# First attention's output projection as three fp32r products over a split context, with the low part formed by VectorE

## What is computed

```
x   = x + tanh(g_xattn[0]) * attn(layernorm(x), ctx, ctx)
q   = Q @ Wq + bq ; k = K @ Wk + bk ; v = V @ Wv + bv      (256 -> 256, split in 16 heads of 16)
out = softmax(q k^T / 4) v                                  (per head)
attn = out @ Wo + bo                                        (256 -> 256: the output projection)
```

## Time and profile before

| what | value |
|---|---|
| median of 3 runs | 870.87 us (869.88 to 871.38) |
| the profiled execution's own time | 870.99 us |
| its span | 868.9 us |
| mean granted TensorE clock | 0.973 |
| PE busy | 800.8 us, 92% |
| DVE busy | 660.6 us, 76% |
| ACT busy | 591.8 us, 68% |
| POOL busy | 129.3 us, 15% |
| first attention | from the start to about 198.6 us |

### The profile page before, as it was taken

One profiled execution on the slowest core, in us unless ns is written; L12 is line 12 of the kernel. 1 busy time (PEld: TensorE's weight loads), 2 busy tenths in 40 slices (PEclk: granted clock), 3 DMA queues, 4 the chain that ended last, 5 costly groups with the idle time before them and its releaser, 6 DMA issues. The chain is left out here.

```text
span 868.9 us, 15644 instructions
## 1 busy us (share of the span) xinstructions
PE 800.8 (92%) x5417; PEld 646.1 (74%) x5419; DVE 660.6 (76%) x1511; ACT 591.8 (68%) x1224; POOL 129.3 (15%) x234
## 2 busy tenths in 40 slices
PE   5799999997877999999999999999999999996767
PEld 5577777665545887888888888888888888885223
DVE  5688888885884878877876876876876876765587
ACT  4377767665625777777777777777777777775663
POOL 4333333320000001000000000000000000000546
PEclk9699999999989999999999999999999999999788
DMA  4734443305005000000000000000000000000002
GB/s 130 134 119 143 139 128 108 102 14 159 1 0 167 13 1 1 13 1 1 13 2 1 13 1 1 14 1 2 14 1 1 1 1 1 1 2 0 1 1 97
DMA packets 40301, 33.49 MB, mean 39 GB/s; under 512 B 12624, under 2 KB 38800, under 8 KB 39968
## 3 DMA queue, kind: packets, MB, share of 16 engines
q1 hardware_dynamic: 37728, 31.63, 12.4%
q0 software_dynamic: 2496, 0.87, 0.7%
HBM read 17.46 MB, written 2.10 MB: 23 GB/s over the span
## 5 line engine op out<-in xcount | busy, mean ns | idle before, releaser
L1923 DVE TENSOR_REDUCE c_neg_max<-c_pS 128x1 f32<-128x512 f32 x128 | 88.3, 690 | 62.8 <-PE c_pS L2178 60.7
L1754 ACT ACTIVATE c_probs<-c_pS,c_neg_max 128x512 f32<-128x512 f32 x128 | 88.1, 688 | 58.7 <-DVE c_neg_max L1923 58.7
L566 DVE TENSOR_REDUCE a_neg_max<-a_pS 128x2 f32<-128x512 f32 x128 | 82.4, 687 | 28.4 <-PE a_pS L813 27.8
L1772 ACT ACTIVATE c_probs<-c_probs,c_r_sum 128x512 f32<-128x512 f32 x128 | 92.5, 722 | 3.9 <-DVE c_r_sum L1929 2.7
L410 ACT ACTIVATE a_probsT<-a_pT 128x512 f32<-128x512 f32 x128 | 70.3, 609 | 25.7 <-PE a_pT L826 25.3
L1907 DVE TENSOR_TENSOR c_pT_lo<-c_pT,c_pT_hi 128x512 fp32r<-128x512 f32 x128 | 87.1, 681 | 0.0
L2139 PE MATMUL c_pK<-c_kv,w_hi 128*128 128x512 f32 x256 | 80.6, 396 | 4.6 <-PEq L1591 4.0
L2195 PE MATMUL c_pO<-c_pT_hi,c_v_hi 128*128 128x256 f32 x256 | 77.7, 304 | 4.2 <-DVE c_pT_lo L1907 4.2
L2165 PE MATMUL c_pK<-w_hi,c_kv 128*128 128x512 f32 x248 | 79.3, 401 | 1.9 <-DVE c_k_lo L1891 1.9
L2185 PE MATMUL c_pT<-ident,c_probs 128*128 128x128 f32 x512 | 76.6, 272 | 0.0
L2185 PEld LDWEIGHTS c_pT<-ident,c_probs 128*128 128x128 f32 x512 | 63.4, 140 | 17.3 <-ACT c_probs L1772 0.6
(11 more groups left out here) (399 smaller groups left out, 2044.0 us busy)
## 6 DMA issues: line engine op xcount, KB each, us to landing
a_q_stack<-w_hi SPq DMA_DIRECT2D x94, 64.0 KB, 2.6
a_k_stack<-w_hi SPq DMA_DIRECT2D x48, 64.0 KB, 2.6
c_kv<-w_hi SPq DMA_DIRECT2D x42, 64.0 KB, 2.6
s_ctx<-in_ctx_dram SPq DMA_DIRECT2D x8, 256.0 KB, 3.7
x_sb<-in_x_dram SPq DMA_DIRECT2D x8, 256.0 KB, 4.2
b_raw<-in_L_xattn_Wkv_dram SPq DMA_DIRECT2D x1, 2048.0 KB, 10.8
ctx_in<-in_ctx_dram SPq DMA_DIRECT2D x8, 256.0 KB, 2.7
out_dram<-x_sb SPq DMA_DIRECT2D x8, 256.0 KB, 2.1
```

Source lines behind the costliest of these rows:

```text
L566: nc.vector.tensor_reduce(neg_max[:, r // 2 % 2, :, e, r % 2], pS[:, e, :, :], AX_X, ALU.max, negate=True).then_inc(s["max"], 1)
L1754: nc.scalar.activation(probs[:, u % 2, :], pS[:, u % 2, :], ACT.Exp, bias=neg_max[:, u % 4:u % 4 + 1], accum_out=sums[:, u % 4:u % 4 + 1]) ...
L1772: nc.scalar.mul(probs[:, u % 2, :], probs[:, u % 2, :], r_sum[:, u % 4:u % 4 + 1]).then_inc(s["probs"], 1)
L1923: nc.vector.tensor_reduce(neg_max[:, u % 4:u % 4 + 1], pS[:, u % 2, :], AX_X, ALU.max, negate=True).then_inc(s["max"], 1)
```

## The change

In batches 0 to 6 the output projection becomes three fp32r products for each contraction block, as in the other projections. `wo` is split once: ACT writes its high part (`wo_high`, at the end of r 7 of batch 0), DVE its low part (`wo_low`, in r 1 of batch 1, in the place where later batches do out_bias). For each batch ACT's copy to `oT_norm` now rounds to fp32r, and a new DVE operation, `onT_low`, subtracts it from bank pP. It stands in r 6 behind q_low in batches 1 to 6, and behind `slot_small` in batch 7. `out_project` waits for it and issues 12 matmuls in place of 4. `onT_out` also waits until the last projection has been done. The last batch's own projection stays float32 and takes its context from a piece of `v_ones` that is free by then. New tiles lie in memory that was already there.

```diff
--- before.py
+++ after.py
@@ -140,7 +140,11 @@
         oT = sb("a_oT", [P, 2, H0 // HG, T])
         r_sum = sb("a_r_sum", [P, TT, H0])
         o_norm = sb("a_o_norm", [P, TT, D])
-        oT_norm = sb("a_oT_norm", [P, DC * T])
+        oT_norm = sb("a_oT_norm", [P, DC * T], F32R)
+        oT_norm_lo = part(1, 5376, 512)
+        oT_last = flat(v_ones[:, 0, :, :, :].rearrange("p t h e -> p t (h e)"))[:, 0:DC * T]
+        wo_hi = [part(1, 4864 + D * c, D) for c in range(DC)]
+        wo_lo = [part(1, 5888, D), part(1, 4096, D)]
         out_b = sb("a_out_b", [P, TT, D])
 
         unit = out_b[0:2, 0, :]
@@ -155,7 +159,7 @@
         pK = pb("a_pK", [P, 512])
         pV = pb("a_pV", [P, 512])
 
-        names = """bvw bvo bo bias x0 x1 x2 x ident ident0 first_k first_q gate load_k load_q load_v load_b load_g load_o ctx next wk wq wv scale
+        names = """wo_hi wo_lo onT_lo bvw bvo bo bias x0 x1 x2 x ident ident0 first_k first_q gate load_k load_q load_v load_b load_g load_o ctx next wk wq wv scale
                    const ones zeros unit units stats moments var rstd xn cT cT_hi cT_lo xT xT_hi xT_lo k k_hi k_lo q q_hi
                    q_lo stack0 stack1 v vb S max parts turned shift shifted0 shifted1 ST exp PV oT oQ rsum on onT onT_sb wo ob res
                    small wT wT_act wT_dve hs tau mean c1 bias1 bvx gh_pre slot_stats slot_moments slot_var slot_rstd slot_xn
@@ -429,8 +433,15 @@
                     act.wait_ge(s["turned"], b * 4 + g + 4)
                 nc.scalar.copy(oT[:, par, g, :], pO[:, 0, :]).then_inc(s["oT"], 1)
 
+            def wo_high():
+                act.wait_ge(s["load_o"], 2 * DMA)
+                for c in range(DC):
+                    last = nc.scalar.copy(wo_hi[c], wo[:, c, :])
+                last.then_inc(s["wo_hi"], 1)
+
             def onT_out(m):
                 act.wait_ge(s["onT"], m + 1)
+                wait(act, s["wo"], m)
                 nc.scalar.copy(oT_norm[:, :], pP[:, :]).then_inc(s["onT_sb"], 1)
 
             def weight_out(i):
@@ -463,6 +474,8 @@
                         v_out(b + 1, 1 - par)
                     if r == 1 and prep:
                         ctxT_hi(b + 2, par, pV)
+                    if r == NR - 1 and b == 0:
+                        wo_high()
                     if r % 2 and not more:
                         weight_out(r - 1)
 
@@ -497,7 +510,7 @@
             weight_out(NTURN - 1)
             for t in range(TT):
                 act.wait_ge(s["onT"], B + t)
-                nc.scalar.copy(oT_norm[:, :].rearrange("p (c t) -> p c t", c=DC)[:, :, t * P:(t + 1) * P],
+                nc.scalar.copy(oT_last.rearrange("p (c t) -> p c t", c=DC)[:, :, t * P:(t + 1) * P],
                                onT_bank(t).rearrange("p (c t) -> p c t", c=DC)).then_inc(s["onT_sb"], 1)
 
         @block.vector
@@ -573,6 +586,16 @@
                 dve.wait_ge(s["rsum"], 2 * m + t + 1)
                 nc.vector.tensor_tensor(o_norm[:, t, :].rearrange("p (h d) -> p h d", d=DK), o[:, :, 0:DK],
                                         r_sum[:, t, :, None].broadcast_to([P, H0, DK]), ALU.mult).then_inc(s["on"], 1)
+
+            def wo_low():
+                dve.wait_ge(s["wo_hi"], 1)
+                for c in range(DC):
+                    last = nc.vector.tensor_tensor(wo_lo[c], wo[:, c, :], wo_hi[c].bitcast(F32), ALU.subtract)
+                last.then_inc(s["wo_lo"], 1)
+
+            def onT_low(m):
+                dve.wait_ge(s["onT_sb"], m + 1)
+                nc.vector.tensor_tensor(oT_norm_lo, pP[:, :], oT_norm[:, :].bitcast(F32), ALU.subtract).then_inc(s["onT_lo"], 1)
 
             def out_bias(m):
                 dve.wait_ge(s["wo"], m + 1)
@@ -660,6 +683,7 @@
                 weight_out(1)
                 residual(b - 2)
                 slot_small()
+                onT_low(b - 1)
                 weight_out(3)
                 slot_sums(1, 0)
                 slot_sums(1, 1)
@@ -685,6 +709,8 @@
                             norm_stats(b + 2)
                             norm_moments(b + 2)
                     if r == 1:
+                        if done and not old:
+                            wo_low()
                         if old:
                             out_bias(b - 2)
                         if prep:
@@ -704,6 +730,8 @@
                         k_low(b + 2, par)
                     if r == 6 and prep:
                         q_low(b + 2, par)
+                    if r == 6 and done:
+                        onT_low(b - 1)
                     if not prep and r in (0, 2):
                         slot_sums(0, r // 2)
                     if not prep and r == 4:
@@ -872,13 +900,16 @@
                 turn(pP, o_norm, "onT")
 
             def out_project(m):
-                pe.wait_ge(s["onT_sb"], m + 1)
-                if isinstance(m, int) and m == 0:
-                    pe.wait_ge(s["load_o"], 2 * DMA)
+                pe.wait_ge(s["onT_lo"], m + 1)
+                if m == 0:
+                    pe.wait_ge(s["wo_lo"], 1)
                 for t in range(TT):
+                    i = 0
                     for c in range(DC):
-                        last = nc.tensor.matmul(pP[:, t * D:(t + 1) * D], oT_norm[:, c * T + t * P:c * T + (t + 1) * P], wo[:, c, :],
-                                                start=(c == 0), stop=(c == DC - 1))
+                        for w, v in ((wo_hi, oT_norm[:, :]), (wo_hi, oT_norm_lo), (wo_lo, oT_norm[:, :])):
+                            last = nc.tensor.matmul(pP[:, t * D:(t + 1) * D], v[:, c * T + t * P:c * T + (t + 1) * P], w[c],
+                                                    start=(i == 0), stop=(i == 3 * DC - 1))
+                            i += 1
                 last.then_inc(s["wo"], 1)
 
             def weight_turn(i):
@@ -922,7 +953,7 @@
             def last_out_project(t):
                 pe.wait_ge(s["onT_sb"], B + t)
                 for c in range(DC):
-                    last = nc.tensor.matmul(out_bank(t)[:, 0:D], oT_norm[:, c * T + t * P:c * T + (t + 1) * P], wo[:, c, :],
+                    last = nc.tensor.matmul(out_bank(t)[:, 0:D], oT_last[:, c * T + t * P:c * T + (t + 1) * P], wo[:, c, :],
                                             start=(c == 0), stop=(c == DC - 1))
                 last.then_inc(s["wo"], 1)
```

## The result

| | before | changed |
|---|---|---|
| median, first timing (8 runs each) | 871.19 us (869.88 to 872.80) | 874.22 us (873.04 to 877.58) |
| ratio, 95% interval | | 1.0044 [1.0029, 1.0058] |
| profiled execution, its span | 870.99, 868.9 us | 873.04, 870.9 us |
| from batch 1's first shifted scores to the next stage's first transposition ("the rounds") | 145.05 us | 147.17 us |
| the span less the rounds ("the rest") | 723.85 us | 723.73 us |

A forecast was written before the change was run, and what follows sets the result against it. PE's list in written order was taken to set the first attention's pace. Stalls of 2.40 and 0.65, less 0.33, plus 0.10 gave +2.82 us on the profiled 870.99, 873.8; the median lies 0.12 lower, so 873.7 us, range 871.4 to 875.3.

The forecast's parts named there:

- The matmuls: Output projection on PE: twelve fp32r matmuls take 1.59 us in place of 1.92, saving 0.33 us each time.
- onT_low's own time: New DVE subtraction on 128x512: 0.681 us, starting behind q_low where the residual started.
- From its end to PE: From the end of onT_low to PE's first matmul of the projection: 0.14 us.
- Batch 3: Counted like batches 2, 4 and 5: PE stalls 0.93 us at the projection, net 0.60 us later.
- Batch 6: No q_low there, so onT_low is ready before PE arrives: no stall, -0.33 us.
- Batch 7: onT_low stands behind slot_small; PE saves 0.33 us, but DVE is the bound: +0.1 in place of -0.33.
- wo's split: ACT's two copies and DVE's two subtractions, once: both hidden; without cover 0.25 and 0.87 us.
- DVE has over 3 us idle in a batch. I count nothing.: DVE's added work pushes residual, pair_max and moments by about 0.60 us: no cost elsewhere counted.
- the argument that PE is as late as DVE: Next batch's first scores: PE and DVE both come about 0.60 us later, so the gap between them stays.
- no stall: Rival: onT_low done before PE reaches the projection; six savings, DVE adds 0.1: -1.9, 869.0 us. Chance 0.12.
- The knock-on: Rival: PE's first scores of the next batch wait for DVE's maxima, up to 0.3 us five times: 875.2 us. Chance 0.08.

The follow-up runs named there:

- e10: The kernel before, unchanged, traced and timed again: rounds 144.92 us, median 870.68 us.
- e11: The kernel before, unchanged, traced and timed once more: rounds 144.92 us, median 869.64 us.
- e5: Changed kernel, high part of the context taken twice, DVE's subtraction kept on other data with nobody waiting: rounds 146.55 us, 874.78 us, ratio 1.0040 to the kernel before.
- e2: Changed kernel with onT_low moved ahead of q_low in round 6: rounds 146.78 us, median 874.52 us, ratio 1.0040 to the kernel before.
- e1: The changed kernel again, no edit: rounds 147.14 us, median 873.98 us, ratio 1.0035 to the kernel before.
- e3: Changed kernel without onT_low or its wait, high part of the context taken twice, still twelve matmuls: rounds 144.01 us, 870.82 us, ratio 0.9996 to the kernel before.
- e6: Changed kernel with the residual moved from round 7 to the front of round 6: rounds 147.17 us, 875.29 us, ratio 1.0041 to the kernel before.
- e7: Changed kernel with both onT_low ahead of q_low and the residual early in round 6: rounds 144.30 us, 871.04 us, ratio 0.9999 to the kernel before.
- e12: Changed kernel without onT_low (high part taken twice), residual moved to the front of round 6: rounds 143.79 us, 872.08 us in one run, kernel before 869.71.
- e9: Changed kernel with the residual early in round 6 and q_low moved behind round 7's pair_max: rounds 152.20 us, 879.32 us, ratio 1.0091 to the kernel before.
- e4: Kernel before plus DVE's subtraction and PE's wait for it, float32 matmuls kept, wo not split: rounds 149.00 us, 877.02 us, ratio 1.0068 to the kernel before.
- e8: Kernel before with only the residual moved to the front of round 6: rounds 144.72 us, 870.64 us, ratio 1.0007 to the unedited kernel before.

## Why the prediction was right

The sign, the mechanism and the size of the time held: a wait of PE ahead of the projection, released by onT_low, in batches 1 to 5 and in no other, and the stage later by some 2 to 3 us. Step by step:

- *The matmuls*: 1.61 us measured for 1.59, so the saving was 0.31 and not 0.33. The estimate from the count of passes in the Trainium skill (FP8 and Floating Point Precision, TensorE Precision Notes), 1.44, was too low; three passes cost 0.84 of the float32 form here, by 1.61 over 1.92.
- *onT_low's own time*: 0.680 for 0.681, and DVE began it 0.07 us before q_low's record ended, so the residual's place was the right one to read. It took 0.60 us of DVE's list (92.14 to 92.74). The rule of the Trainium skill that I had weighed against the rows (VectorE: DVE Perf Modes, The DRAIN you can't avoid) did not show; the same section says that a next operation that nothing holds starts earlier, and with that the trace agrees, by these 0.07 us.
- *From its end to PE*: the term that was mis-sized. I took 0.14 from a projection whose first instruction waits; here it is 0.05. That is 0.09 in five batches, 0.45 of the 0.70 us by which the sum was too high.
- *Batch 3*: +0.37 in place of 0.60. The kernel before had lost 0.15 us there at the scores of round 1 (97.19 to 97.68 in place of 0.34), in all three of its traces, which the changed kernel has not. I had taken four batches as alike from their clocks at the projection alone.
- *Batch 6*: -0.45 for -0.33. In the first trace of the kernel before two instructions of round 2 took 0.15 us more than elsewhere (159.84 to 160.67 for two times 0.34); why is not known. e10 and e11 do not have it, with 17.84 and 17.83 for this batch, and against them the change gives -0.3, as forecast.
- *Batch 7*: +0.01 for +0.10. As forecast, nothing of PE's 0.31 us reached the end.
- *wo's split*: hidden, as forecast. ACT made the copies in 0.73 us behind batch 0's exponentials, and the next exponential began 0.67 after them with no wait of PE. In the changed kernel:

```profile
52.59 0.73 ACT L439 CAST w_lo<-a_wo 128x256 fp32r<-128x256 f32 x2
53.26 1.08 ACT L414 ACTIVATE a_probsT<-a_pT 128x512 f32<-128x512 f32 x2
...
55.65 0.75 DVE L593 TENSOR_TENSOR w_lo<-a_wo,w_lo 128x256 fp32r<-128x256 f32 x2
```

What I had wrong without its showing in the number is the sentence "DVE has over 3 us idle in a batch. I count nothing." In the changed kernel nothing came on top of the wait, but only just: PE came 0.85 - 0.31 = 0.54 us later in batch 2 and DVE's list was 0.60 longer, so the argument that PE is as late as DVE was off by 0.06, which was all the room there was. That it was enough was luck. The list was no cover: e5 shows that the operation costs 1.5 us without any wait. And the rival "no stall" was priced at -1.9 us; e2, which is that case, came out 1.7 us above the kernel before in its rounds. A rival's price has to be worked out through the next bound as well. The knock-on, to which I gave 0.08, is the mechanism that stood ready behind the forecast.

That the forecast of 873.7 meets the median of 874.22 so closely is luck in part: the sum was 0.7 too high for the rounds, and the medians are some 1 us further apart than the rounds.

## What to carry to other kernels

An idle share says little of an engine: what counts is how much room its list has between the instruction that releases it and the one that waits for its last result, and here that was 0.06 of 20 us. Where an operation is added at such a place, removing the wait on it gives little until the list behind it is shortened as well; look for both before judging either. Before moving an operation back, follow all its readers, DMA queues among them.

## What the runs showed of the hardware

The end of the DVE operation and the first matmul that waits for it are 0.05 us apart in the changed kernel, 0.06 at the scores of e2, and 0.14 in the rows of project_k. What makes the difference was not tried.

The granted clock behind the barrier differs from run to run of the same code. Busy time by stretch (the third number from the end is the granted clock), of the changed kernel and then of the kernel before:

```profile
199.00:204.00 5.00, 4.17 (x18) 3.80 (x19) 2.90 (x12) 3.14 (x6) 1.21 (x4) 0.66 0.58 198
200.00:201.00 1.00, 1.00 (x6) 1.00 (x6) 1.00 (x4) 1.00 (x1) 0.00 (x0) 0.50 0.40 37
```

```profile
199.00:204.00 5.00, 4.47 (x28) 3.23 (x27) 3.01 (x13) 3.74 (x7) 1.01 (x1) 1.00 0.82 313
```

In both PE had been idle 2.34 us at the barrier, and the clock goes down to 0.50, the 1.2 GHz level, in the one and stays at 2.4 GHz in the other. The next stage's first work then takes 205.81 - 199.83 = 5.98 us in place of 203.84 - 198.67 = 5.17, 0.81 us more. e1, the same kernel, stays at full clock there. Of fourteen traces seven show it: those of the changed kernel's first run, e2, e3, e5, e6, e7 and e12; it is not in e1 and e9, nor in the five of the kernel before and its variants (its first, e4, e8, e10 and e11). The same code at the barrier can thus go either way, and yet it fell on the changed kernel and its variants alone, on seven traces of nine; were it blind to the kernel, a split as uneven as this would come up about once in a hundred times (7 of 14, all among 9: 36 in 3432). When the barrier falls does not sort them: the next stage starts at 196.9 to 202.0 us in the seven and at 197.7 to 206.8 in the others. By its 0.81 us it could make most of the 1 us by which the medians are further apart than the rounds, though the two first traces, one with it and one without, have rests of 723.73 and 723.85. Whether the change brings it about stays open.

Beside the rounds, the rest of the fourteen traces runs from 722.6 us at a mean clock of 0.974 (e3) to 727.7 at 0.965 (e5), with the same code in all: more than the change itself moves.

The timed runs show the same. Among the runs of the kernel before, the time falls by 0.3 to 0.4 us for each 0.001 of mean granted clock. If the runs of a kernel and those of the kernel before beside it are brought to one clock by a common straight line, an estimate, the mean difference for e1 goes from 2.9 to 2.5 us (within 0.6), for e2 from 3.4 to 1.8, for e5 from 3.6 to 1.1 and for e7 from +0.5 to -0.3. In the rounds these are 2.1, 1.7, 1.5 and -0.7. The line is crude: for e4 it gives 5.1 (4.0 in the rounds) and for e9 5.9 (7.2). But most of what the times of e1, e2, e5 and e7 show beyond the rounds goes with the clock. Why the runs of e2 and e5 have a lower mean clock (0.968 and 0.967 against 0.973) was not tried.
